# A four-layer modulated convolution folded into one kernel per sample: the order of the opening's loads and sums, low parts against GpSimd, one store behind copies, and the last sample in two banks

## Chip, core and metric

The kernel runs on one core of one Trainium2 chip. The metric is the device time of one execution in microseconds (us), the median of repeated runs. A profile of one execution is read with it; its time line starts at the first instruction.

## What is computed

The input is x, 128 samples of 64 channels by 1024 positions, and a style vector of 128 numbers per sample. Four convolution layers of 64 channels and three taps follow each other, each with weights that depend on the sample:

```python
s = style @ mw.T + mb                                   # per sample and input channel
weight = SCALE * w * s[:, None, :, None]
demod = lax.rsqrt(jnp.sum(weight * weight, axis=(2, 3)) + EPS)
weight = weight * demod[:, :, None, None]
# types: 'same', 'upsample' (transposed conv, stride 2, then blur),
#        'same', 'downsample' (blur, then stride 2); each adds its bias b
x = x + L0(x, cond_512, ...)
```

Everything is linear, so the four layers of a sample fold into one short filter, plus a constant and a correction at the ends of the sequence.

## The kernel before

**Filters.** For each group of four samples (g = 0 to 31) TensorE multiplies small matrices in seven units, `unit(g, u)`, u = 0 to 6: units 0 and 1 are the root products (Q3 by A2), 2 and 3 bring in B1, 4 to 6 bring in C. Their results are in PSUM banks `pg`. Between units VectorE scales a result with per-sample factors (`full`, L914, L916, L922, L931), ScalarE rounds it to the 32-bit format that TensorE takes at full rate (`high`, L624, L628) and VectorE forms the rest as a second such number (`low`, L939 to L949). Each product is thus three matmuls, high by high, high by low, low by high (`split_mm`, L182 to L184). The last units give the filter Wf with seven tap matrices (S0, W0, W1, S2, W2, W3, W4), whose high and low parts go into W (`w_high`/`w_low`, for group 0 and the first pair of it `pair_high`/`pair_low`, L643 and L1019). Nine SP transfers per group (`cross`, L231) copy parts of W to the other half of the partitions, each as soon as `s_wh` and `s_wl` say that the parts are ready.

**Samples.** For each sample b, `conv_shared(b)` makes a sum of three taps that both output halves share into `ps` (or a `pg` bank), 9 matmuls of 256 columns. ScalarE copies it twice into `py` (`shared_copy`, L592), `conv_rest(b)` adds five taps in 15 matmuls, and ScalarE writes the scaled result into T (`result`, L600). The input comes in pairs of samples n = b // 2: SP's `load(n)`, GpSimd's two differences (`columns(n)`, L846 and L847), ScalarE's high part (`x_high`, L586), and the low part (`x_low`) on GpSimd for the first three pairs (L851), on VectorE for the others (L906). T has two halves: `result` of pair n waits until `store(n - 2)` has landed. Samples 120 to 127 (from LAST) have no more units behind them; for the last group the copies are made in halves (`last_cross`).

**Order.** All queues are written out by hand, engine by engine; an engine runs its list in order and waits on semaphores. SP has one queue for loads, copies and stores. In the loop over groups (L287) it issues a load, a store, the nine copies of the next group, a load and a store. The opening works the same way: SP and ACT load constants; TensorE forms style products (`scale`, L477), energies (`energy`, L481) and the B1 sums (L499, in fp32, with the identity and three multiples of it that GpSimd makes at L813); ScalarE takes squares and roots (L659, L664), VectorE does three Newton steps on each root (`newton`, L1014 to L1017). `JUNK` matmuls (L529) fill the time before the first sample. VectorE's list ahead of the loop is L1059 to L1161.

## Time and profile before

| | us |
|---|---|
| median of 3 runs | 629.14 (628.71 to 630.32) |
| the profiled execution | 630.22 |
| its span | 628.4 |
| TensorE busy | 617.2 (98%) |
| VectorE busy | 527.8 (84%) |
| ScalarE busy | 437.2 (70%) |
| GpSimd busy | 243.4 (39%) |
| DMA queue of SP | 75.0% of 16 engines |

The span reaches from the first to the last instruction; the execution's own time has some 1.8 us more around it. A matmul's time in the profile contains its way through the pipeline, so rows of 0.28 us start every 0.12 us; whether TensorE loses time is seen from the starts. "Idle before" names what ended a wait, "issue" where no record of the profile does.

### The profile page before, as it was taken

Reading aid. Unit: us, or ns where it says so; the run is one execution under the profiler, and the core shown is the slowest. Engines: PE = TensorE matmul, PEld = TensorE weight load, DVE = VectorE, ACT = ScalarE, POOL = GpSimd, SP = SyncE. Lnnn points to the kernel's source line nnn. Section 1 sums busy time; section 2 is a strip of 40 time slices with the busy share of each in tenths; the row PEclk is TensorE's granted clock in tenths of the full one; section 3 lists DMA queues with packets and bytes.
Section 4 is the critical chain, followed back from the end, with each engine's and each line's share of the span. In section 5 each row is a group of like instructions: output and inputs, shape, how many; then the busy total and the mean of one; then the engine's idle time right before and its main releaser. Section 6 shows DMA issues by size and latency. Waiting matters only on the chain.

```text
span 628.4 us, 13021 instructions
## 1 busy us (share of the span) xinstructions
PE 617.2 (98%) x4849; PEld 603.8 (96%) x4849; DVE 527.8 (84%) x783; ACT 437.2 (70%) x730; POOL 243.4 (39%) x251
## 2 busy tenths in 40 slices
PE   8998999999999999999999999999999999999997
PEld 7888999999999999999999999999999999999997
DVE  5989878899988888888898887889788888888881
ACT  6658776767776776766776777676767677676673
POOL 5556434424424423433423433432442443343430
PEclk9999999999999999999999999999999999999999
DMA  6448977778968677887678787777897877798683
GB/s 195 133 105 207 251 190 205 214 196 217 243 173 235 203 223 199 228 220 188 209 210 230 205 227 206 204 220 200 206 252 166 237 204 220 197 239 219 188 234 136
DMA packets 154287, 129.38 MB, mean 206 GB/s; under 512 B 7025, under 2 KB 120625, under 8 KB 154225
## 3 DMA queue, kind: packets, MB, share of 16 engines
q1 hardware_dynamic: 153920, 128.29, 75.0%
q8 instruction: 39, 0.64, 0.4%
q10 hardware_dynamic: 304, 0.26, 0.2%
q14 instruction: 24, 0.19, 0.1%
HBM read 36.44 MB, written 33.75 MB: 112 GB/s over the span
## 4 chain that ended last, share of the span: by engine, by line
PE 94%; DVE 2%; ACT 1%; issue 1%; DMA 1%; POOL 0%; ACTq 0%; DVEq 0%
PE py L183 12%; PE py L184 12%; PE py L182 12%; PE pg L182 8%; PE pg L184 8%; PE pg L183 8%; PE ps L182 7%; PE ps L183 7%; PE ps L184 7%; PE pg L187 3%; PE pg L188 3%; PE pg L409 1%; PE pg L410 1%; PE pe L465 1%; DMA EYE<-in_eye 1%
## 5 line engine op out<-in xcount | busy, mean ns | idle before, releaser
L183 PE MATMUL py<-xl,W 128*128 128x256 f32 x640 | 181.7, 284 | 0.0
L184 PE MATMUL py<-xh,W 128*128 128x256 f32 x640 | 181.4, 283 | 0.0
L182 PE MATMUL py<-xh,W 128*128 128x256 f32 x640 | 181.1, 283 | 0.0
L846 POOL TENSOR_TENSOR X<-X 128x514 f32<-128x514 f32 x64 | 74.3, 1161 | 217.3 <-DMA X<-in_xin 199.2
L182 PEld LDWEIGHTS py<-xh,W 128*128 128x128 f32 x640 | 126.2, 197 | 0.2 <-issue 0.2
L184 PEld LDWEIGHTS py<-xh,W 128*128 128x128 f32 x640 | 126.1, 197 | 0.0
L183 PEld LDWEIGHTS py<-xl,W 128*128 128x128 f32 x640 | 125.6, 196 | 0.0
L592 ACT COPY py<-ps 128x512 f32<-128x512 f32 x123 | 70.5, 573 | 60.9 <-PE ps L184 60.5
L906 DVE TENSOR_TENSOR xl<-X,xh 128x1548 fp32r<-128x1548 f32 x61 | 108.2, 1773 | 1.1 <-ACT xh L586 1.0
L182 PE MATMUL ps<-xh,W 128*128 128x256 f32 x369 | 105.2, 285 | 1.8 <-issue 1.8
L183 PE MATMUL ps<-xl,W 128*128 128x256 f32 x369 | 104.8, 284 | 0.0
L184 PE MATMUL ps<-xh,W 128*128 128x256 f32 x369 | 104.6, 283 | 0.0
L600 ACT ACTIVATE T<-py,cv,DD 128x512 f32<-128x512 f32 x128 | 99.8, 779 | 6.3 <-PE py L184 6.3
L586 ACT CAST xh<-X 128x1548 fp32r<-128x1548 f32 x64 | 94.8, 1482 | 0.0
L847 POOL TENSOR_TENSOR X<-X 128x516 f32<-128x516 f32 x64 | 84.4, 1319 | 0.0
L830 POOL TENSOR_TENSOR Q3l<-Q3f,Q3h 128x256 fp32r<-128x256 f32 x31 | 24.4, 786 | 140.4 <-ACT Q3h L615 140.4
L182 PEld LDWEIGHTS ps<-xh,W 128*128 128x128 f32 x369 | 72.5, 196 | 2.4 <-issue 2.4
L635 ACT CAST W<-Wf 128x768 fp32r<-128x768 f32 x60 | 50.3, 839 | 33.8 <-PE py L184 24.4
L963 DVE TENSOR_TENSOR W<-Wf,W 128x768 fp32r<-128x768 f32 x60 | 67.4, 1149 | 7.1 <-ACT W L635 6.7
L183 PEld LDWEIGHTS ps<-xl,W 128*128 128x128 f32 x369 | 72.7, 197 | 0.0
L184 PEld LDWEIGHTS ps<-xh,W 128*128 128x128 f32 x369 | 72.6, 197 | 0.0
L628 ACT CAST Gh<-pg 128x512 fp32r<-128x512 f32 x64 | 37.8, 591 | 35.3 <-DVE pg L916 35.3
(194 smaller groups left out, 1416.3 us busy)
## 6 DMA issues: line engine op xcount, KB each, us to landing
X<-in_xin SPq DMA_DIRECT2D x64, 516.0 KB, 5.5
out<-T SPq DMA_DIRECT2D x63, 512.0 KB, 4.3
W<-W SPq DMA_DIRECT2D x60, 384.0 KB, 4.4
W<-W SPq DMA_DIRECT2D x93, 128.0 KB, 4.2
W<-M SPq DMA_DIRECT2D x90, 128.0 KB, 3.6
W<-W SPq DMA_DIRECT2D x30, 256.0 KB, 4.7
W<-W SPq DMA_DIRECT2D x7, 192.0 KB, 2.8
E<-in_ed SPq DMA_DIRECT2D x1, 768.0 KB, 7.7
```

Source lines behind the costliest of these rows:

```text
L182: eng.matmul(o, wh_, rh, start=first, stop=False, skip_group_check=onto)
L183: eng.matmul(o, wh_, rl, start=False, stop=False, skip_group_check=onto)
L184: return eng.matmul(o, wl_, rh, start=False, stop=last, skip_group_check=onto)
L586: act.copy(xh[:, n % XH], X[:, n % XR, :, 1:4]).then_inc(s_xh, 1)
L592: act.copy(py[b % YR][:, :].rearrange("p (e k) -> p e k", e=2), shared(b).unsqueeze(1).to_broadcast([128, 2, H])).then_inc(s_ae, 1)
L600: act.activation(T[:, n % TR, q].rearrange("p e k -> p (e k)"), py[b % YR][:, :], ACT.Identity, bias=cv[:, b:b + 1], scale=DD[:, L[3], b:b ...
L628: act.copy(Gh[:, :, 2 * u - 4:2 * u - 2], src).then_inc(s_gh, 1)
L635: act.copy(taps_of(g, 0, k), Wf[:, :, PARTS[k]]).then_inc(s_wh, 1)
L846: pool.tensor_tensor(x[:, :, 3, 0:XW - 1], x[:, :, 0, 1:XW], x[:, :, 1, 0:XW - 1], ALU.subtract)
L847: pool.tensor_tensor(x[:, :, 2], x[:, :, 0], x[:, :, 1], ALU.subtract).then_inc(s_s, 1)
L906: tt(xl[:, n % XH], X[:, n % XR, :, 1:4], r32(xh[:, n % XH]), ALU.subtract).then_inc(s_xl, 1)
L963: m = tt(taps_of(g, 1, k), Wf[:, :, PARTS[k]], r32(taps_of(g, 0, k)), ALU.subtract)
```

## The change

- **Loads of the opening.** b1 goes from fourth to second place on SP, eye from third to second on ACT.
- **Opening sums.** TensorE does the two scale products of layers 0 and 1 after the B1 sums, ScalarE the first root ahead of the second square, ScalarE and VectorE the B1 parts ahead of what needs those scale products; one Newton step moves ahead of the product of `full(0, 2)`.
- **First samples.** One of the two copies for the first tap goes out on ACT's queue; `first_shared` does the first tap of sample 0, then of sample 1, then the others. 10 filler matmuls, not 13.
- **Low parts.** The three `pair_low(1, k)` stand together, ahead of the wait for PP_K2; `w_low(1, 0)` stands behind `full(1, 6)`; `D10` stands later. GpSimd does `q3_low(2)` ahead of `x_low(1)` and then waits for `s_wl` to reach 4 before `columns(2)`. ScalarE does `q3_high(2)` and `q3_full(3)` earlier.
- **Near the end.** At g = 29 SP issues the nine copies and load(62) ahead of store(57).
- **Last sample.** Its shared sum is copied in two halves, into `py` and `ps`; results and stores of the halves are separate.

VectorE from the last low part of the root product of group 1 to the scaling of the filter. The names: Q2h high part and rest of the root product, W and M the low parts of the filter, kt and tmp the constant's, pg the products of unit 2 and 3, Wf the filter. Before:

```order
L191 TENSOR_TENSOR Q2h<-pg,Q2h 64x2x128
L1023 TENSOR_TENSOR W<-Wf,W 128x3x128
L1131 SCALAR_TENSOR_TENSOR kt<-pe,DD 64x128
L1132 SCALAR_TENSOR_TENSOR tmp<-kt,MS,S 64x128
L1023 TENSOR_TENSOR W<-Wf,W 128x3x128
L1025 TENSOR_TENSOR M<-Wf,M 128x128
L916 TENSOR_TENSOR pg<-pg,D10c 128x512 x2
```

and now:

```order
L191 TENSOR_TENSOR Q2h<-pg,Q2h 64x2x128
L1040 TENSOR_TENSOR W<-Wf,W 128x3x128 x2
L1042 TENSOR_TENSOR M<-Wf,M 128x128
L1149 SCALAR_TENSOR_TENSOR kt<-pe,DD 64x128
L1150 SCALAR_TENSOR_TENSOR tmp<-kt,MS,S 64x128
L933 TENSOR_TENSOR pg<-pg,D10c 128x512 x2
```

The second W part and the M part moved ahead of the two steps that wait for TensorE's constant.

SP in the turn of g = 29 and the start of g = 30, as the difference (X<-in_xin is a load, out<-T a store, the others copy W):

```order
 L228 DMA out<-T 128x2x512
 L223 DMA X<-in_xin 128x2x516
-L228 DMA out<-T 128x2x512
-L238 DMA W<-W 64x12x128
-L239 DMA W<-W 64x4x128
-L240 DMA W<-W 64x4x128
-L242 DMA W<-W 64x12x128
-L243 DMA W<-W 64x4x128
-L244 DMA W<-W 64x8x128
-L223 DMA X<-in_xin 128x2x516
-L246 DMA W<-M 64x4x128
```

```order
+L246 DMA W<-M 64x4x128
+L247 DMA W<-M 64x4x128
+L248 DMA W<-M 64x4x128
+L223 DMA X<-in_xin 128x2x516
+L228 DMA out<-T 128x2x512 x2
 L223 DMA X<-in_xin 128x2x516
```

The store that stood ahead of the copies now stands behind them and behind load(62), next to store(58).

```diff
@@ -27 +27 @@
 LAST = B - 2 * NG
-JUNK = 13
+JUNK = 10
 EPS = 1e-8 * (C * 9)
@@ -211 +211 @@
     for n, dst, src in (("m2", MS[:], m2),
+                        ("b1", b1w, b1.rearrange("p (s c) -> p s c", s=4)),
                         ("m301", M301, m301),
                         ("q3", q3s[:], q3.rearrange("p (k o) -> p k o", k=2)),
-                        ("b1", b1w, b1.rearrange("p (s c) -> p s c", s=4)),
                         ("a2", A2f, a2)):
@@ -282 +282 @@
     sp.dma_start(w[hi, S0:W1 + 1, :, 0, 1], w[lo, S0:W1 + 1, :, 0, 0]).then_inc(s_w0, 16)
-    sp.dma_start(w[lo, S0, :, 0, 1], w[hi, W0, :, 0, 0]).then_inc(s_w0, 16)
     sp.dma_start(w[lo, W1, :, 0, 1], w[hi, W0, :, 0, 0]).then_inc(s_w1, 16)
@@ -293 +292 @@
             last_cross(0)
-        if n:
+
+        late = g + 3 == NGR
+        if n and not late:
             store(n - 1)
@@ -298 +299 @@
         elif g + 1 < NGR:
-            cross(g + 1, 0)
-            cross(g + 1, 1)
-
-            if g == NGR - 3:
-                load(n + 1 + XR)
-            cross(g + 1, 2)
-        if n + 1 + XR < NQ and g != NGR - 3:
+            for k in range(3):
+                cross(g + 1, k)
+        if n + 1 + XR < NQ:
             load(n + 1 + XR)
+        if late:
+            store(n - 1)
         store(n)
@@ -311 +310 @@
     n = NQ - 1
-    for q in range(Q):
-        sp.wait_ge(s_y, Q * n + q + 1)
-        sp.dma_start(out[n * Q + q], T[:, n % TR, q]).then_inc(s_st[n % TR], 16)
+    for k, (q, e) in enumerate(((0, slice(0, 2)), (1, 1), (1, 0))):
+        sp.wait_ge(s_y, Q * n + k + 1)
+        sp.dma_start(out[n * Q + q][:, e], T[:, n % TR, q, e]).then_inc(s_st[n % TR], 16)
...
@@ -332 +331 @@
 -                if b == 0:
...
-            return
        if g == NGR - 1 and q == 0:
@@ -361 +344 @@
             pe.wait_ge(s_xl, n + 1)
-        if b > LAST or b == 2:
-            pe.wait_ge(s_ae, b - 1)
-        elif b == 1:
-            pe.wait_ge(s_ce, PLACE[0, 6] + 1)
-        elif b:
-            pe.wait_ge(s_ae, b)
+        pe.wait_ge(s_ae, b - 1 if b > LAST or b == 2 else b)
         taps(b, shared(b), XO, ((S0, True, False), (S2, False, False), (W4, False, True))).then_inc(s_a, 1)

+    def first_shared():
+
+        o = [shared(b) for b in range(Q)]
+        pe.wait_ge(s_h0, 1)
+        pe.wait_ge(s_l0, 1)
+        pe.wait_ge(s_w0, 16 * 2)
+        pe.wait_ge(s_xh, 1)
+        pe.wait_ge(s_xl, 1)
+        taps(0, o[0], XO, ((S0, True, False),))
+        pe.wait_ge(s_ce, PLACE[0, 6] + 1)
+        taps(1, o[1], XO, ((S0, True, False),))
+        pe.wait_ge(s_h0, 2)
+        pe.wait_ge(s_l0, 2)
+        pe.wait_ge(s_vh, 1)
+        pe.wait_ge(s_vl, 1)
+        taps(0, o[0], XO, ((S2, False, False),), k=1)
+        pe.wait_ge(s_vh, 2)
+        pe.wait_ge(s_vl, 2)
+        taps(0, o[0], XO, ((W4, False, True),), k=2).then_inc(s_a, 1)
+        taps(1, o[1], XO, ((S2, False, False), (W4, False, True)), k=1).then_inc(s_a, 1)
+
     def conv_rest(b):
@@ -374 +373 @@
             pe.wait_ge(s_vl, 3)
-        o = py[b % YR]
-        taps(b, o[:, H:2 * H], XO1, ((W1, False, False), (W3, False, True)), True)
-        taps(b, o[:, 0:H], XE0, ((W0, False, False), (W2, False, False), (W4, False, True)), True).then_inc(s_p, 1)
+        o = [py[b % YR][:, 0:H], py[b % YR][:, H:2 * H]]
+        if b == B - 1:
+            o[0] = ps[:, 0:H]
+        m = taps(b, o[1], XO1, ((W1, False, False), (W3, False, True)), True)
+        if b == B - 1:
+            m.then_inc(s_p, 1)
+            pe.wait_ge(s_ae, b + 2)
+        taps(b, o[0], XE0, ((W0, False, False), (W2, False, False), (W4, False, True)), True).then_inc(s_p, 1)

@@ -490 +494 @@
     scale(3, M301[:, 0:128]).then_inc(s_pp, 1)
-    scale(0, M301[:, 128:256])
-    scale(1, M301[:, 256:384]).then_inc(s_pp, 1)

@@ -500 +502 @@
     m.then_inc(s_pp, 1)
+    scale(0, M301[:, 128:256])
+    scale(1, M301[:, 256:384]).then_inc(s_pp, 1)
     for x in PROLOGUE[:2]:
@@ -529 +533 @@
         pe.matmul(py[i % YR][:, :], A2h[:, 0:128], A2h[:, :], start=True, stop=True)
-    conv_shared(0)
-    conv_shared(1)
+    first_shared()
     conv_rest(0)
@@ -577 +580 @@
     act.dma_start(WT[:, 0], wt2.rearrange("p (t m) -> p t m", t=3)).then_inc(s_in["wt2"], 16)
-    act.dma_start(WT[:, 1:4], wt.rearrange("p (l t m) -> p l t m", l=3, t=3)).then_inc(s_in["wt"], 16)
     act.dma_start(EYE[:], eye).then_inc(s_in["eye"], 16)
+    act.dma_start(WT[:, 1:4], wt.rearrange("p (l t m) -> p l t m", l=3, t=3)).then_inc(s_in["wt"], 16)

@@ -672 +675 @@
     act.activation(tmp[0:64, L[2]], scales[2][0:64], ACT.Square, bias=BB[0:64, 1, 2:3]).then_inc(s_ss, 1)
-    act.wait_ge(s_in["wt"], 16)
-    square(1, 4)
     act.wait_ge(s_pp, PP_E2)
     root(RR[:, L[2]], pe_[:, 0:128])
+    act.wait_ge(s_in["wt"], 16)
+    square(1, 4)
     act.wait_ge(s_in["a2"], 16)
@@ -683 +686 @@
     m.then_inc(s_q3h, 1)
-    act.wait_ge(s_pp, PP_S01)
-    for l in (2, 1):
-        act.activation(S[:, l], scales[l], ACT.Identity, bias=BB[:, 1, l:l + 1]).then_inc(s_sa, 1)
     act.wait_ge(s_pp, PP_B1)
@@ -690 +690 @@
              py[0][:, 0:5 * C].rearrange("p (m c) -> p m c", m=5).unsqueeze(2).to_broadcast([128, 5, 2, C])).then_inc(s_k0, 1)
+    act.wait_ge(s_pp, PP_S01)
+    for l in (2, 1):
+        act.activation(S[:, l], scales[l], ACT.Identity, bias=BB[:, 1, l:l + 1]).then_inc(s_sa, 1)
     for l in (0, 1):
@@ -713 +716 @@
     act.copy(W[lo, 0, W2, 0, 0, 1], Wf[hi, 0, W1])
+    act.wait_ge(s_h0, 1)
+    act.wait_ge(s_l0, 1)
+    act.dma_start(r32(W[lo, 0, S0, :, 0, 1]), r32(W[hi, 0, W0, :, 0, 0])).then_inc(s_w0, 16)
     pair_high(0, 1)
@@ -728 +734 @@
     x_high(1)
+    q3_high(2)
     high(1, 2)
     high(1, 3)
-    q3_high(2)
+    q3_full(3)
     act.wait_ge(s_sc, SC_CV)
@@ -744 +751 @@
     high(2, 1)
-    q3_full(3)
     q3_high(3)
@@ -795 +801 @@
         result(b - 2)
-        shared_copy(b)
+        if b < B - 1:
+            shared_copy(b)
+
+    b = B - 1
+    act.wait_ge(s_a, b + 1)
+    act.wait_ge(s_y, b - YR + 1)
+    act.copy(py[b % YR][:, H:2 * H], shared(b)).then_inc(s_ae, 1)
+    act.copy(ps[:, 0:H], shared(b)).then_inc(s_ae, 1)
     result(B - 2)
-    result(B - 1)
+    for k, (e, o) in enumerate(((1, py[b % YR][:, H:2 * H]), (0, ps[:, 0:H]))):
+        act.wait_ge(s_p, b + 1 + k)
+        act.activation(T[:, b // Q % TR, b % Q, e], o, ACT.Identity, bias=cv[:, b:b + 1],
+                       scale=DD[:, L[3], b:b + 1]).then_inc(s_y, 1)

@@ -868 +884 @@
     identity(1)
-    x_low(1)
     q3_low(2)
+    x_low(1)
+    pool.wait_ge(s_wl, 4)
     for b in range(B):
@@ -1052 +1069 @@
         full(g, 5)
-        w_low(g, 0)
         dve.wait_ge(s_id, g + 1)
@@ -1057 +1073 @@
         full(g, 6)
+        w_low(g, 0)

@@ -1081 +1098 @@
     lone_low(dve, Q3h[hi, :, 1], Q3f[hi, :, 1]).then_inc(s_q3l, 1)
-    dve.wait_ge(s_sa, 2)
-    reached(tt(D21[:], S[:, 1], S[:, 2], ALU.mult))
     dve.wait_ge(s_k0, K_B1)
@@ -1088 +1103 @@
        r32(B1hw[:, C:11 * C]).rearrange("p (m h c) -> p m h c", m=5, h=2), ALU.subtract).then_inc(s_b1, 1)
+    dve.wait_ge(s_sa, 2)
+    reached(tt(D21[:], S[:, 1], S[:, 2], ALU.mult))
     dve.wait_ge(s_sc, SC_D21)
@@ -1100 +1117 @@
     link(newton(0, 2, py[0][:, 0:128], ps[:, 256:384]))
+    link(newton(1, 2, None, ps[:, 256:384]))
     dve.wait_ge(s_k, 1)
     full(0, 2)
-    link(newton(1, 2, None, ps[:, 256:384]))
     link(newton(2, 2, None, ps[:, 256:384]))
@@ -1128 +1145 @@
     low(1, 1)
-    pair_low(1, 0)
+    for k in range(3):
+        pair_low(1, k)
     dve.wait_ge(s_pp, PP_K2)
@@ -1132 +1150 @@
     reached(stt(out=tmp[lo, 2], in0=kt[lo], scalar=BB[lo, 0, 2:3], in1=S[lo, 3, :], op0=ALU.add, op1=ALU.mult))
-    pair_low(1, 1)
-    pair_low(1, 2)
     full(1, 2)
@@ -1147 +1163 @@
     w_low(1, 2)
-    tt(D10[:], DD[:, L[0]], DD[:, L[1]], ALU.mult)
     dve.wait_ge(s_k0, K_B0)
@@ -1160 +1175 @@
     low(3, 1)
+    tt(D10[:], DD[:, L[0]], DD[:, L[1]], ALU.mult)
     dve.wait_ge(s_xl, 3)
```

## Rows read from the trace of the kernel before

**Rows 1.** The page, part 1: busy time, share of the span, instructions of each engine.

```profile
PE 617.2 (98%) x4849; PEld 603.8 (96%) x4849; DVE 527.8 (84%) x783; ACT 437.2 (70%) x730; POOL 243.4 (39%) x251
```

**Rows 2.** Timeline of the opening: start, us, engine, line, operation [idle before, releaser].

```profile
7.03 1.06 PE L477 MATMUL ps<-MS,Wf 128*128 128x128 f32 x4
8.40 0.77 PE L499 MATMUL py<-b1s,EYE 128*128 128x128 f32 x2 [0.32 <-POOL Wf L813]
11.38 0.56 PE L182 MATMUL pg<-Q3h,A2h 128*128 128x256 f32 x1
...
6.54 1.71 POOL L813 TENSOR_SCALAR Wf<-EYE 128x128 f32<-128x128 f32 x3 [4.40 <-DMA EYE<-in_eye]
```

**Rows 3.** DMA issues by line: engine, operation, number, size, median us to landing.

```profile
W<-W SPq DMA_DIRECT2D x7, 192.0 KB, 2.8
W<-W SPq DMA_DIRECT2D x11, 64.0 KB, 2.5
...
out<-T SPq DMA_DIRECT2D x2, 256.0 KB, 2.0
...
EYE<-in_eye ACTq DMA_DIRECT2D x1, 64.0 KB, 4.5
```

**Rows 4.** Timeline before the first tap sum, TensorE and SP.

```profile
24.46 3.13 PE L529 MATMUL py<-A2h 128*128 128x512 f32 x13
28.00 0.37 PE L182 MATMUL ps<-xh,W 128*128 128x256 f32 x1 [0.41 <-issue]
...
25.29 0.63 SPq L283 DMA_DIRECT2D W<-W  x1
```

**Rows 5.** Timeline from 33 to 50 us, TensorE, VectorE and GpSimd.

```profile
39.60 0.47 PE L182 MATMUL pg<-Gh,Ch 128*128 128x512 f32 x1 [0.61 <-DVE Gl L945]
...
49.22 0.36 PE L182 MATMUL pg<-Q2h,B1h 128*128 128x256 f32 x1 [1.65 <-DVE Q2h L191]
...
34.22 3.29 DVE L1025 TENSOR_TENSOR M<-Wf,M 128x128 fp32r<-128x128 f32 x1
...
43.06 1.86 DVE L963 TENSOR_TENSOR W<-Wf,W 128x768 fp32r<-128x768 f32 x1
...
33.63 3.73 POOL L851 TENSOR_TENSOR xl<-X,xh 128x1548 fp32r<-128x1548 f32 x1 [0.57 <-ACT xh L586]
...
43.00 1.10 POOL L847 TENSOR_TENSOR X<-X 128x516 f32<-128x516 f32 x1
```

**Rows 6.** Timeline from 584 to 603 us, TensorE, VectorE, ScalarE and SP.

```profile
601.07 0.37 PE L182 MATMUL ps<-xh,W 128*128 128x256 f32 x1 [1.39 <-issue]
...
584.38 1.81 DVE L963 TENSOR_TENSOR W<-Wf,W 128x768 fp32r<-128x768 f32 x2
...
595.83 0.79 ACT L600 ACTIVATE T<-py,cv,DD 128x512 f32<-128x512 f32 x1
596.50 1.48 ACT L586 CAST xh<-X 128x1548 fp32r<-128x1548 f32 x1
599.78 0.92 ACT L656 CAST W<-Wf 128x384 fp32r<-128x384 f32 x2 [1.79 <-DVE Wf L958]
...
602.45 0.57 ACT L592 COPY py<-ps 128x512 f32<-128x512 f32 x1 [1.07 <-PE ps L184]
...
586.63 0.60 SPq L238 DMA_DIRECT2D W<-W  x1
...
596.38 0.60 SPq L228 DMA_DIRECT2D out<-T  x1
```

**Rows 7.** Timeline of SP, the first copy of the group before, at g = 28.

```profile
567.11 0.60 SPq L238 DMA_DIRECT2D W<-W  x1
```

**Rows 8.** The store behind those copies and a load, issued at 576.6: landing.

```profile
DMA to landing us min/median/max: 5.5/5.5/5.5
```

**Rows 9.** All 56 stores issued from 60 to 580 us: landing.

```profile
DMA to landing us min/median/max: 2.9/4.7/6.5
```

**Rows 10.** Timeline of ScalarE, the last result.

```profile
625.16 0.78 ACT L600 ACTIVATE T<-py,cv,DD 128x512 f32<-128x512 f32 x1 [1.03 <-PE py L184]
```

More of the change, by code:

```diff
@@ L163, in build @@
             sem(n) for n in ("pp", "ch", "eps", "ms", "sq", "ss", "rr", "sc", "k0", "b1", "j", "ey", "vh", "vl", "k"))
-        PP_S2, PP_E2, PP_S3, PP_S01, PP_B1, PP_E01, PP_E3, PP_K1, PP_K2, PP_K3 = range(1, 11)
+        PP_S2, PP_E2, PP_S3, PP_B1, PP_S01, PP_E01, PP_E3, PP_K1, PP_K2, PP_K3 = range(1, 11)
         SC_S3, SC_D32, SC_D21, SC_D, SC_K2, SC_K3, SC_CV = range(1, 8)
@@ L311, in _ @@
             n = NQ - 1
-            for q in range(Q):
-                sp.wait_ge(s_y, Q * n + q + 1)
-                sp.dma_start(out[n * Q + q], T[:, n % TR, q]).then_inc(s_st[n % TR], 16)
+            for k, (q, e) in enumerate(((0, slice(0, 2)), (1, 1), (1, 0))):
+                sp.wait_ge(s_y, Q * n + k + 1)
+                sp.dma_start(out[n * Q + q][:, e], T[:, n % TR, q, e]).then_inc(s_st[n % TR], 16)
             for i in range(TR):
-                sp.wait_ge(s_st[i], 16 * (len(range(i, NQ, TR)) + (Q - 1 if i == n % TR else 0)))
+                sp.wait_ge(s_st[i], 16 * (len(range(i, NQ, TR)) + (2 if i == n % TR else 0)))
             sp.wait_ge(s_eo, 16)
@@ L332, in conv_shared @@
                 n, q = divmod(b, Q)
-                if b == 0:
-                    pe.wait_ge(s_h0, 1)
-                    pe.wait_ge(s_l0, 1)
-                    pe.wait_ge(s_w0, 16 * 2)
-                    pe.wait_ge(s_xh, 1)
-                    pe.wait_ge(s_xl, 1)
-                    taps(b, shared(b), XO, ((S0, True, False),))
-                    pe.wait_ge(s_h0, 2)
-                    pe.wait_ge(s_l0, 2)
-                    pe.wait_ge(s_vh, 1)
-                    pe.wait_ge(s_vl, 1)
-                    taps(b, shared(b), XO, ((S2, False, False),), k=1)
-                    pe.wait_ge(s_vh, 2)
-                    pe.wait_ge(s_vl, 2)
-                    taps(b, shared(b), XO, ((W4, False, True),), k=2).then_inc(s_a, 1)
-                    return
                 if g == NGR - 1 and q == 0:
@@ L577, in _ @@
             act.dma_start(WT[:, 0], wt2.rearrange("p (t m) -> p t m", t=3)).then_inc(s_in["wt2"], 16)
+            act.dma_start(EYE[:], eye).then_inc(s_in["eye"], 16)
             act.dma_start(WT[:, 1:4], wt.rearrange("p (l t m) -> p l t m", l=3, t=3)).then_inc(s_in["wt"], 16)
-            act.dma_start(EYE[:], eye).then_inc(s_in["eye"], 16)
             def x_high(n):
@@ L672, in _ @@
             act.activation(tmp[0:64, L[2]], scales[2][0:64], ACT.Square, bias=BB[0:64, 1, 2:3]).then_inc(s_ss, 1)
+            act.wait_ge(s_pp, PP_E2)
+            root(RR[:, L[2]], pe_[:, 0:128])
             act.wait_ge(s_in["wt"], 16)
             square(1, 4)
-            act.wait_ge(s_pp, PP_E2)
-            root(RR[:, L[2]], pe_[:, 0:128])
             act.wait_ge(s_in["a2"], 16)
@@ L868, in _ @@
             identity(1)
+            q3_low(2)
             x_low(1)
-            q3_low(2)
+            pool.wait_ge(s_wl, 4)
             for b in range(B):
```

## The prediction

> **What bounds the kernel now.** I read the page first. TensorE's matmul row is busy for 98% of the span [rows 1], and its granted clock is in the top tenth in all 40 slices of the page (the 2.4 GHz level), so time can only go where TensorE's issue is interrupted, before its stream starts, or after its last matmul. The waits view shows only a handful of entries for it, so I went through the TensorE timeline and looked for matmuls that start more than 0.12 us after the one before (0.12 us is the regular step of the 256-column ones). After the opening there are four interruptions: first tap sum at 28.00, first matmul of sample 1's product at 39.60 (0.61 idle), root product at 49.22 (1.65 idle, 1.80 against the regular step) and first shared sum of sample 120 at 601.07 (1.39 idle, 1.54 against the step) [rows 4 to 6]. Between 49.22 and 599.5 there is none. A gain before 49.22 therefore shifts everything behind it, if what the other engines and the DMAs deliver moves with it.
>
> **Term A: the opening, 0.35 us.** The B1 sums (L499) start at 8.40 [rows 2], released by GpSimd's three scaled identities, which waited for EYE. EYE was issued as ACT's third transfer and took 4.5 us; a 64 KB transfer elsewhere takes 2.5 [rows 3]. It is now second, one issue of some 0.6 us earlier, at 1.3, so it should land at 3.8 to 5.8, and GpSimd's 1.71 us follow. Then B1 can start where the two scale products of layers 0 and 1 started, at 7.03, and these (1.06 us) follow it. The step from 8.40 to the first root product at 11.38 is 2.98 us; 7.03 + 2.98 + 0.96 (1.06 less the overlap of two neighbours) = 10.97, 0.4 earlier. A little of that may be lost where more of the root product runs before the clock is up: its matmuls there step by 0.2 us, later ones by 0.12. VectorE's B1 low part and products follow TensorE there; one Newton step now fills VectorE's wait before the next product. Ends: 0 (m301, now behind b1, or wt, now behind EYE, lands late and holds the scale product or a square) and 1.0 (all of 8.40 minus 7.03, less what B1's own chain needs). I take 0.35, near the sum.
>
> **Term B: first tap sum, 0.42 us.** Two copies gate it, issued by SP one after the other; the second goes out at 25.29 and takes 2.5 us, 27.8, and TensorE starts at 28.00 [rows 3, 4]. Now ACT issues that copy at 24.6, beside SP's first; the first (192 KB, 2.8 us) is then last, at 27.4. The gain is 0.4. ACT's issue costs its queue 0.6 us before pair_high(0,1), which itself waits for VectorE there until 25.76: hidden. The ends are 0.1 and 0.45. The Trainium skill, "DMA: Bandwidth & Descriptors", section "Issuing engines are not separate DMA queues", speaks against more: transfers issued from several engines run on the same 16 DMA engines and interleave, so only issue time is saved. By that page the second copy's 64 KB would push out the first's landing, and B would be nearer 0.1. Three filler matmuls fewer (0.24 each) cost nothing while TensorE waits for this copy: fillers end at 24.46 - 0.35 + 2.5 = 26.6, the data is there at 27.2. Sample 1's first taps ahead of sample 0's second fill the time until the low parts are ready, worth no more than 0.1, and are counted at nothing.
>
> **Term C: 0.77 us, the wait at 39.60.** VectorE's M<-Wf,M at L1025 took 3.29 us for 128 columns; it starts at 34.22 and ends with GpSimd's xl at 33.63 + 3.73 [rows 5]. The products at L916 queue behind it, then ScalarE's high parts and the low ones, and TensorE waits 0.61. The change puts all three pair_low(1,k) before the wait on PP_K2, so they run near 31.4 to 33.0, ahead of that xl, which also moves behind q3_low(2). Then L916 waits for its own product only and is done by 36.0; TensorE arrives at 37.9 with everything there. I book 0.61 idle plus the restart, 0.77, whole.
>
> **Term D: 1.0 us of the 1.80 at 49.22.** Here the chain is VectorE's: from the product at 39.60, through L922, L963, L957, L931, L914 to the low part that releases TensorE. In it L963 starts at 43.06 and takes 1.86; GpSimd's columns end at 43.00 + 1.10 = 44.10, 1.04 later [rows 5]. The new wait on s_wl holds these columns until VectorE has done its low part, now after full(1,6). The chain loses 1.0 and keeps the rest: TensorE, which was there at 49.22 - 1.80 = 47.42, now is at 47.42 - 0.35 - 0.42 - 0.77 = 45.88, and is released at 49.22 - 1.54 - 1.0 = 46.68. So 0.8 of the wait stays. Queued behind GpSimd's new wait are columns(2), q3_low(3) and x_low(2); sample 4 needs the last at about 56.4, and columns end near 46.6 and x_low(2) near 50: covered by 6 us. Ends: 0.5 and 1.3.
>
> **Term E: the copies ahead of a store, a loss of 0.5 us.** The wait at 601.07 is for the last of nine W copies of group 30. At g = 29 SP now leaves store(57) and load(62) until these are issued: the first goes when its low part is ready, halfway through the L963 pair of 584.38 and so near 585.35, instead of at 586.63 [rows 6], and two transfers of half a megabyte are out of its way. I expect the last to land near 598, a little before TensorE wants it at 599.5, and the 1.54 us to go. But store(57) frees the half of T that result(118) writes. That result started at 595.83 [rows 6]. In group 28 the step from the first copy's issue at 567.11 to the landing of the store behind copies and load is 576.6 + 5.5 - 567.11 = 15.0 us [rows 7, 8]; with one store less ahead I allow 13.5 to 15. So store(57) lands at 598.9 to 600.4, and result(118) waits 3 to 4.5 us. Behind it on ScalarE are x_high(61), two last_high (0.92), result(119) and shared_copy(120), and TensorE's rest of sample 120 waits for that copy: 0.67 + 1.38 + 0.83 + 0.70 + 0.57 + 0.15 for the signal = 4.3 us from result(118)'s start (each row's time less the tenth by which the next overlaps it), so 603.2 to 604.7. Before, that rest started at 601.07 + 2.26 (18 matmuls and a restart) = 603.33. The edit is worth between +0.1 and -1.4; with the landing at 599.5 it costs 0.5. What is late next is the rest of sample 120, for a store's landing and no longer for copies. Ends: a gain of 1.54, a loss of 1.4.
>
> **Term F: the tail, 0.3 us.** The last result (0.78 us [rows 10]) is halved, its first half runs beside the last nine matmuls, in its own bank. At most 0.39 is saved, less the fixed part; the last store is half as large, but its 2.0 us [rows 3] is already short of what the 64 KB copies take. I take 0.3, ends 0.1 and 0.6. The copy of shared(127) in two is ready before it is wanted.
>
> **Sum.** 0.35 + 0.42 + 0.77 + 1.0 - 0.5 + 0.3 = 2.34 us. The profiled execution took 630.22 us (span 628.4, 1.8 around it), so a profile of the change should show a span near 626.1. That execution is 1.1 above the median of the runs, 629.14; from the median I get **626.8 us**. About 0.3%, 1.9 us, is what a measurement of this kernel can tell from no change: 627.25 is the border.
>
> **Rivals.**
> *The store lands in time* (chance 0.12). If store(57) lands by 597.4, result(118) costs TensorE nothing and E is +1.54 instead of -0.5: 629.14 - 4.4 = 624.8. For it: 56 stores took 2.9 us at the least [rows 9], and issued at 594.5 that would do. Against: this one is behind nine copies and a load, and their median is 4.7.
> *The lock moves instead of going* (0.13). VectorE's w_low(1,1), w_low(1,2) and edge_in near 46.6 to 49 now meet GpSimd's q3_low(3) and x_low(2). If edge_in falls behind x_low(2), over 3 us long as the xl row in [rows 5], full(2,2) comes near 52, and TensorE waits about 1.7 us at the product of group 2: 628.5. The M row above is just such a case. The Trainium skill, "SBUF — State Buffer", section "Who interferes with whom", says that a VectorE instruction with two SBUF inputs and a GpSimd one that reads SBUF block each other for a whole instruction, whoever is first; edge_in and w_low have two such inputs. By that page it hangs on tenths of a microsecond who wins; the row of M agrees with it.
> *The opening gives nothing* (0.18). m301 or wt lands late, A and half of B fall away: 629.14 - 1.8 = 627.3.
> *Slower than before* (0.07): the stall of term E is larger. It decides from the point where store(57) lands after 601.8, since each microsecond beyond 599.0 goes straight to TensorE, and the other terms give 2.84. Issued at 596.38, where SP now has the store after those copies [rows 6], and landing in 6.5 us, the longest of the stores [rows 9], it would be 602.9, E -3.9: 629.14 - 2.84 + 3.9 = 630.2. Against it: with a store and a load fewer ahead SP should be there about two issues sooner.
> The forecast's own case has 0.50; its range alone is 625.8 to 627.8.
>
> **How the numbers follow.** Faster by more than the border: most of the forecast's case (0.40), all of the first rival, half of the third's 0.18 and a little of the lock's: 0.64. Within it: 0.31. Slower: the far part of the last rival and what I overlook, 0.05. The range 624.7 to 628.6 takes in the early store and the lock, and leaves out the slower case and the ends where several terms fail together.
>
> **What would show it.** A: B1 sums start near 7.1. B: first tap sum near 27.2. C: no VectorE row of 128 columns above 1 us before 40, and no idle before sample 1's products. D: L963's successor takes under 1 us, idle before the root product falls from 1.65 to about 0.7 and sits near 46.7. E: no "issue" wait before sample 120's shared sum, but a gap of 1 to 3 us before its rest, and ScalarE idle before result(118), released by the store. F: last activation 0.5 us. The forecast is wrong if the stream between these points is no longer gapless, if the clock rises later than before, or if the root product comes later than 47.5.

## Result and profile after

The changed kernel takes 632.77 us (median of 22 runs, 628.33 to 634.32), the kernel before 629.18 (22 runs, 628.21 to 630.32): ratio 1.0049, 95% interval 1.0035 to 1.0063. It is 3.6 us slower where 2.3 us less were forecast, and it lies above the range (624.7 to 628.6). The profiled execution took 632.22 us, span 630.3.

The page, part 1, of the changed kernel [rows 1 before]:

```profile
PE 616.7 (98%) x4846; PEld 602.6 (96%) x4846; DVE 530.7 (84%) x783; ACT 437.2 (69%) x732; POOL 242.5 (38%) x251
```

TensorE is as busy as before; the two microseconds are waits again. The waits view of the changed kernel, TensorE alone (what waited, for what: us in total, times, longest):

```profile
PE py L182 <- ACT py L595: 2.8, 1, 2.8
PE pg L182 <- DVE Gl L962: 1.7, 2, 0.9
...
PE ps L182 <- issue: 1.4, 2, 1.2
PE pe L462 <- DVE b1s L987: 1.2, 1, 1.2
PE pg L182 <- DVE Q2h L191: 1.0, 2, 0.6
```

Of the lines shown, two have no counterpart before: the first, and L462's for b1s. The timeline of TensorE at the points of the terms (a line of the kernel before is up to 17 higher here):

```profile
7.17 0.77 PE L501 MATMUL py<-b1s,EYE 128*128 128x128 f32 x2
10.72 0.36 PE L182 MATMUL pg<-Q3h,A2h 128*128 128x256 f32 x1
27.08 0.36 PE L182 MATMUL ps<-xh,W 128*128 128x256 f32 x1 [1.17 <-issue]
46.53 0.36 PE L182 MATMUL pg<-Q2h,B1h 128*128 128x256 f32 x1 [0.63 <-DVE Q2h L191]
52.05 1.24 PE L462 MATMUL pe<-b1s,E 128*128 128x192 f32 x6 [1.21 <-DVE b1s L987]
54.21 0.47 PE L182 MATMUL pg<-Gh,Ch 128*128 128x512 f32 x1 [0.92 <-DVE Gl L962]
56.99 0.38 PE L413 MATMUL pg<-Gh,Ch 128*128 128x256 f32 x1 [0.21 <-DVE Q2l L956]
605.63 0.39 PE L182 MATMUL py<-xh,W 128*128 128x256 f32 x1 [2.83 <-ACT py L595]
```

Up to 50 us it goes as forecast and better. The root product of group 2 comes at 46.53, 2.69 us before its time in [rows 5] (forecast: 46.68), the wait before sample 1's product is gone, and the one before the root product fell from 1.65 to 0.63. Then TensorE waits three times for VectorE, and the lead of 2.69 becomes a lag of 0.38. The cause is a pair on VectorE and GpSimd:

```profile
47.68 0.96 DVE L982 TENSOR_TENSOR M<-Wf,M 128x256 fp32r<-128x256 f32 x1
48.57 3.43 DVE L987 TENSOR_TENSOR b1s<-XE,S 128x256 f32<-128x256 f32 x1
52.02 1.30 DVE L933 TENSOR_TENSOR pg<-pg,D10c 128x512 f32<-128x512 f32 x2
...
48.44 3.27 POOL L867 TENSOR_TENSOR xl<-X,xh 128x1548 fp32r<-128x1548 f32 x1
```

edge_in (L987) starts 0.13 us after GpSimd's x_low(2) and ends 0.29 us after that ends. In the kernel before it came first and was short (VectorE, then GpSimd):

```profile
51.07 0.41 DVE L970 TENSOR_TENSOR b1s<-XE,S 128x256 f32<-128x256 f32 x1
...
52.16 3.21 POOL L851 TENSOR_TENSOR xl<-X,xh 128x1548 fp32r<-128x1548 f32 x1
```

It is the sight of M in [rows 5], on another instruction. Behind it the product L933, the low parts of G and with them TensorE are late.

From 60 to 585 us the lag stays at 0.38; at 590 it becomes 0.94 in this trace, at a first tap sum of group 29, for which the profile names no cause ("issue", 0.27 us); no term has this loss of 0.56 us, and two other traces of the changed kernel's order at group 29 have one of 0.2 and 0.5 there. The last part, ScalarE and SP (last result and store against [rows 6]):

```profile
601.45 0.78 ACT L603 ACTIVATE T<-py,cv,DD 128x512 f32<-128x512 f32 x1 [4.59 <-DMA out<-T]
602.12 1.47 ACT L589 CAST xh<-X 128x1548 fp32r<-128x1548 f32 x1
603.49 0.92 ACT L659 CAST W<-Wf 128x384 fp32r<-128x384 f32 x2
604.32 0.78 ACT L603 ACTIVATE T<-py,cv,DD 128x512 f32<-128x512 f32 x1
604.99 0.59 ACT L595 COPY py<-ps 128x512 f32<-128x512 f32 x1
...
586.46 0.60 SPq L238 DMA_DIRECT2D W<-W  x1
...
595.82 1.01 SPq L228 DMA_DIRECT2D out<-T  x2
```

The wait of [rows 6] for the last copy is gone. But store 57 goes out at 595.8 and lands 5.5 us later, result(118) waits 4.59 us for it, and the chain of term E follows: TensorE stands 2.83 us at the rest of sample 120. The lag ends at 2.42. After the start of the last matmul 3.04 us are left, before 3.56. So the two profiled executions differ by 2.69 - 3.07 - 0.56 - 1.48 + 0.52 = -1.9 us, which is the whole difference of their spans.

### The profile page after: what moved, and what is told of

It is laid out like the page before. It is cut to its first block, busy times and chain, and to the rows that moved or that the text cites. A ratio compares the mean times of both kernels' runs of the same rounds, so it can differ in the third digit from the quotient of the medians.

```text
span 630.3 us, 13020 instructions
## 1 busy us (share of the span) xinstructions
PE 616.7 (98%) x4846; PEld 602.6 (96%) x4846; DVE 530.7 (84%) x783; ACT 437.2 (69%) x732; POOL 242.5 (38%) x251
## 4 chain that ended last, share of the span: by engine, by line
PE 89%; DVE 5%; ACT 2%; SPq 1%; issue 1%; DMA 1%; ACTq 0%; DVEq 0%
PE py L182 11%; PE py L183 11%; PE py L184 11%; PE pg L182 8%; PE pg L184 8%; PE pg L183 8%; PE ps L182 7%; PE ps L183 7%; PE ps L184 7%; PE pg L187 3%; PE pg L188 3%; PE pg L413 1%; PE pg L414 1%; DMA out<-T 1%; PE pe L469 1%
## 5 line engine op out<-in xcount | busy, mean ns | idle before, releaser
L862 POOL TENSOR_TENSOR X<-X 128x514 f32<-128x514 f32 x64 | 72.7, 1135 | 222.9 <-DMA X<-in_xin 201.8
L846 POOL TENSOR_TENSOR Q3l<-Q3f,Q3h 128x256 fp32r<-128x256 f32 x31 | 25.7, 827 | 134.9 <-ACT Q3h L618 134.9
```

The costliest lines, as they stand in the source:

```text
L862: pool.tensor_tensor(x[:, :, 3, 0:XW - 1], x[:, :, 0, 1:XW], x[:, :, 1, 0:XW - 1], ALU.subtract)
```

## Experiments

Medians of one group of runs stand beside 22 to 27 runs of the kernel before on the same chip (629.25 to 629.48). "Lead" is how much earlier than in the first trace of the kernel before a matmul starts.

### The two stalls, apart and together

The changed kernel once more without an edit (first), with SP's order of group 29 as before (second), with one wait on GpSimd (third), with both (fourth). The wait holds x_low(2) until edge_in is done:

```
                if b == Q:
+                    pool.wait_ge(s_ed, 1)
                    x_low(2)
```

> The changed kernel once more, beside the experiments. Its trace shows two stalls that the kernel before has not: TensorE stands 2.83 us at the rest of sample 120 (released by a store's landing through ScalarE), and from 52 to 57 us it loses 3.07 us because VectorE's scaling of the edge columns takes 3.43 us. Theory S (two additive stalls): runs spread with the landing of that one store, so from about 628 (it lands in 3 us) to 634, mean clock unimportant. Rival K: the stall at the end of the kernel also lets TensorE's granted clock fall for some us; then a run with a mean clock of 1.000 is near 628.5 to 632 and one with 0.997 some 1.5 to 2 us above it, and a trace with 0.997 shows the clock fall next to 603 us. Expected median 632.5.

Measured: 634.14 us (630.49 to 635.08), ratio 1.006 [1.0042, 1.0079]. That is 4.7 us above the kernel before on this chip, where the first comparison had 3.6.

> The changed kernel with the order of SP's transfers at group 29 as before (store 57 ahead of the copies, load before the last copy); all else kept. Theory S: the 2.83 us stall goes and the old wait of 1.39 us at the first tap sum of sample 120 comes back; the trace lost 1.48 us there, so 632.22 - 1.5 = 630.7 for a profile like the last, median about 631.2. Rival K (stall plus clock): 629.2 to 629.7, all runs at a mean clock of 1.000, and a much narrower spread of runs, like the kernel before's. A third view, that the loss from 52 to 57 us is a chance of one execution: below 627.5.

Measured: 630.15 us (627.92 to 631.21), ratio 1.0005 [0.9992, 1.0019]. The wait for the last copy is back (1.05 us); the three waits at 52 to 58 us are there as before, a loss of 3.1.

> The changed kernel plus one wait on GpSimd: its low part of the third pair of samples (3.3 us) starts only after VectorE's first scaling of the edge columns. Theory: the two lock each other; with the wait VectorE's instruction falls to about 0.6 us, the stalls of 1.21, 0.92 and 0.21 us from 52 to 57 us go, TensorE gains 2.5 to 3.1 us: median 629.5 to 630.2. The late stall at the rest of sample 120 stays (2.8 us in a trace). Rival: VectorE's instruction is slow in itself or TensorE waits for the next thing (the low part of sample 4, held longer now): gain under 1 us, median 631.8 or more.

Measured: 630.79 us (628.09 to 631.72), ratio 1.0011 [0.9998, 1.0024]. The three waits are gone from its trace; the late one is there (2.76 us).

> Both edits: SP's order of group 29 as before, and GpSimd's low part behind the edge scaling. If the two stalls are all that went wrong, the sum of my terms without term E and with a gain of 2.5 to 3 us in the opening is left: TensorE 2.7 us ahead at 49 us, old wait at 601, tail 0.5 shorter: 629.2 - 2.7 - 0.5 = 626.0, range 625.5 to 626.7, narrow spread, clock 1.000. If more is lost elsewhere (a clock that falls in the opening because fewer filler matmuls run): 627.5 or more with a mean clock below 1.000.

Measured: 627.82 us (627.07 to 628.79), ratio 0.9967 [0.9955, 0.9979].

Undoing the store's order is worth 4.0 us alone and 3.0 us beside the other edit, the wait on GpSimd 3.4 and 2.3, the two together 6.3, so each is worth 1.0 less once the other is there. Both stalls are real, and without them the change is 1.7 us faster than the kernel before by the medians. The timeline of the kernel with both edits, VectorE and GpSimd:

```profile
49.50 0.41 DVE L988 TENSOR_TENSOR b1s<-XE,S 128x256 f32<-128x256 f32 x1
...
50.05 3.22 POOL L867 TENSOR_TENSOR xl<-X,xh 128x1548 fp32r<-128x1548 f32 x1 [0.75 <-DVE b1s L988]
```

The same instruction takes 0.41 us where it took 3.43, as soon as x_low(2) isn't under way. The timeline marks no wait of TensorE between 48 and 598 us there.

The wait does not remove every lock. In the trace with the wait alone (third run) the pair W<-Wf,W now meets GpSimd's column differences and takes 3.11 us, where the trace with both edits has 1.81; ScalarE and TensorE follow, and TensorE's lead falls from 2.39 to 1.71:

```profile
59.03 3.11 DVE L981 TENSOR_TENSOR W<-Wf,W 128x768 fp32r<-128x768 f32 x2
...
59.52 1.81 POOL L863 TENSOR_TENSOR X<-X 128x516 f32<-128x516 f32 x1
...
63.92 0.40 PE L182 MATMUL py<-xh,W 128*128 128x256 f32 x1 [0.41 <-ACT py L595]
```

Of the six traces with this wait two have that loss, 0.7 and 0.6 us (this one and the first with a third T buffer, below), and four have none: in the trace with both edits it is GpSimd's instruction that is long (2.48 us from 59.95 on).

Part of the loss is TensorE's clock. In the trace of the repeated change (634.18 us) the windows view, TensorE and its granted clock (the column after POOL), reads:

```profile
48.00:52.00 4.00, 2.96 (x25) 2.76 (x24) 4.00 (x2) 0.04 (x1) 3.92 (x3) 1.00 0.74 177
...
54.00:56.00 2.00, 1.66 (x5) 1.41 (x6) 1.94 (x5) 0.32 (x2) 0.70 (x2) 0.60 1.03 133
56.00:58.00 2.00, 2.00 (x9) 1.71 (x9) 1.61 (x5) 2.00 (x7) 0.00 (x0) 0.54 0.98 346
58.00:60.00 2.00, 2.00 (x19) 2.00 (x19) 1.97 (x3) 1.81 (x2) 1.48 (x2) 1.00 0.95 364
...
604.00:606.00 2.00, 0.00 (x0) 0.00 (x0) 1.46 (x3) 2.00 (x5) 0.00 (x0) 1.00 0.00 0
606.00:608.00 2.00, 1.86 (x13) 1.86 (x14) 1.99 (x3) 1.75 (x5) 0.00 (x0) 0.84 0.64 147
608.00:610.00 2.00, 2.00 (x11) 2.00 (x11) 1.46 (x4) 1.18 (x2) 0.42 (x1) 0.50 0.66 149
610.00:612.00 2.00, 2.00 (x16) 2.00 (x15) 0.99 (x1) 1.99 (x4) 1.74 (x2) 0.80 0.61 177
```

After each stall the granted clock goes from 2.4 to 1.2 GHz (1.00 to 0.5) for some 3 us, with 9 and 11 matmuls in 2 us instead of 19. This trace loses 4.0 us from 50 to 60 instead of 3.07, and 2.8 instead of 1.48 at the end. Of the changed kernel's own 22 runs only three have a mean clock of 1.000, the profiled one (632.22 us) among them; the others have 0.997 or 0.994. So the trace that was read first lacks a part of the loss that most runs have. Against rival K of the first expectation, the clock doesn't sort the runs by itself: those at 0.997 took 630.1 to 634.3 us. The two others at 1.000 took 628.33 and 628.51, inside the forecast's range; no trace shows which stalls they were spared.

### Each order edit by itself

The change of group 29 alone, on the kernel before:

```
-                if n:
+
+                late = g + 3 == NGR
+                if n and not late:
                     store(n - 1)
...
-                    cross(g + 1, 0)
-                    cross(g + 1, 1)
-
-                    if g == NGR - 3:
-                        load(n + 1 + XR)
-                    cross(g + 1, 2)
-                if n + 1 + XR < NQ and g != NGR - 3:
+                    for k in range(3):
+                        cross(g + 1, k)
+                if n + 1 + XR < NQ:
                     load(n + 1 + XR)
+                if late:
+                    store(n - 1)
                 store(n)
```

> The kernel before with one edit alone: at group 29 SP issues the three copies and the load ahead of store 57. So far the edit cost 4.0 us in the medians, about 1.5 us in a trace whose clock stayed up and 2.8 in two whose clock fell after the stall. Here TensorE comes 2.5 us later to the place than in the changed kernel with the edge wait, and store 57 hangs on SP's queue, whose times hang on TensorE too, so the stall should be the same: theory (stall of 2.8 us for the 1.39 us one, and the clock falling in most runs): +2 to +3.5 us on the kernel before, 631.5 to 633, mean clock 0.997 in most runs. Rival (the cost comes from an interplay with the other edits): within 0.7 us of the kernel before.

Measured: 631.98 us (630.92 to 632.42), ratio 1.0038 [1.0025, 1.0051]; mean clock of its trace 0.997. The edit alone costs 2.6 us by the medians; the lead in its trace goes from +1.14 before the stall to -0.17 behind it and, with the clock at half (0.50 from 604 to 606 us), to -1.76 at the end. ScalarE and TensorE there:

```profile
599.31 0.78 ACT L600 ACTIVATE T<-py,cv,DD 128x512 f32<-128x512 f32 x1 [4.54 <-DMA out<-T]
...
603.50 0.52 PE L182 MATMUL py<-xh,W 128*128 128x256 f32 x1 [2.79 <-ACT py L592]
```

The next has the store first, all copies, then the load. It is the changed kernel with the wait on GpSimd; against its order of group 29 as before, the edit is:

```
-                    if g == NGR - 3:
-                        load(n + 1 + XR)
                     cross(g + 1, 2)
-                if n + 1 + XR < NQ and g != NGR - 3:
+                if n + 1 + XR < NQ:
                     load(n + 1 + XR)
```

> As the kernel with both edits (627.82), but at group 29 SP issues store 57, then all three copies, then the load; before, the load went out ahead of the last copy. Theory (the wait at the first tap sum of sample 120 is the last copy behind half a megabyte of load): that wait falls from 0.65 to 1.4 us to under 0.3, result(118) does not wait for store 57, gain 0.5 to 1.0: median 626.9 to 627.3. Rival (it waits for the copy because SP comes late to it, held by the store's own wait): no gain, 627.8, the wait stays at 0.65 or more.

Measured: 627.92 us (626.13 to 628.74), ratio 0.9972 [0.9963, 0.9982], no gain over the kernel with both edits (0.9967). Half right: the wait at sample 120 went, and one of 1.0 us came at sample 122. GpSimd and VectorE there:

```profile
598.55 1.37 POOL L858 TENSOR_TENSOR X<-X 128x514 f32<-128x514 f32 x1 [9.65 <-DMA X<-in_xin]
599.89 1.42 POOL L859 TENSOR_TENSOR X<-X 128x516 f32<-128x516 f32 x1
...
600.26 2.67 DVE L920 TENSOR_TENSOR xl<-X,xh 128x1548 fp32r<-128x1548 f32 x1
```

The later load makes GpSimd's column differences late, and they now overlap VectorE's low part (2.67 us; 1.76 in the trace with both edits). That this is what the wait at sample 122 comes from is likely; the profile gives it as "issue".

The new wait on the low parts of group 1, taken out (group 29 as before, no wait for edge_in):

```
-            pool.wait_ge(s_wl, 4)
```

> As the kernel with group 29's order undone (630.15), but without the new wait of GpSimd on the low parts of group 1. Theory (that wait is what pushed GpSimd's third low part onto VectorE's edge scaling): GpSimd runs earlier, VectorE's edge scaling takes about 0.4 us instead of 3.43 and the 3 us of stalls from 51 to 58 us go; in return term D is lost, the root product of group 2 waits about 1 us more: shift of TensorE against the kernel before -0.7 to -1 at 60 us, median 628.2 to 629. Rival (the lock falls on another VectorE instruction in any case, as before at 43 us): 629.5 or more.

Measured: 629.32 us (627.02 to 631.05), ratio 0.9997 [0.9983, 1.001]. Not as either said. In its trace edge_in takes 0.41, x_low(2) waits for ScalarE's x_high(2) and starts at 50.04, and the root product has no wait; instead TensorE waits 1.04 for ScalarE's W parts at 42.5, and from 28 to 50 us it gains 1.3 us (1.8 with the wait and edge_in first). Runs from 627 to 631 in one kernel show that the order isn't fixed here; the trace is one of the good ones. That the bad ones have the lock is likely and not shown. In this trace GpSimd was free for x_low(2) at 49.17, ahead of edge_in at 49.37. It started behind edge_in because x_high(2) came at 48.41, not at 47.28 as in the second run, behind a copy that waited 1.0 us for TensorE. So the new wait isn't what brings x_low(2) forward. The rows say what does: ScalarE's Q3h of group 3 was at 49.38 before and is at 45.37 now, x_high(2) at 50.42 and now 46.42, since q3_full(3) went earlier on ScalarE and TensorE itself was 2.7 us ahead. So x_low(2) went from 52.16 to 48.44, 3.7 us, but VectorE's edge_in, in the middle of its chain, from 51.07 to 48.57, only 2.5: the two met.

SP issues the second copy of group 0 again (term B undone; both stalls undone):

```
+            sp.dma_start(w[lo, S0, :, 0, 1], w[hi, W0, :, 0, 0]).then_inc(s_w0, 16)
...
-            act.dma_start(r32(W[lo, 0, S0, :, 0, 1]), r32(W[hi, 0, W0, :, 0, 0])).then_inc(s_w0, 16)
```

> As the kernel with both edits (627.82), but the second copy of group 0's first tap sum is issued by SP behind its first, as in the kernel before, and not by ScalarE. In four traces of the changed issue the step from the end of the fillers to the first tap sum was 0.1 to 0.2 us longer than before, so the two transfers only share the 16 DMA engines: gain of 0 to 0.3 us in the trace, no difference in the medians (627.5 to 628.1). Rival (my term B): 0.4 us slower at the first tap sum, against the first root product.

Measured: 627.19 us (626.81 to 628.08), ratio 0.9965 [0.9952, 0.9978]. From the first filler to the first tap sum it is 3.57 us here, 3.43 to 3.62 in all seven traces in which SP issues both (mean 3.56), and 3.62 to 3.84 in the seven with ScalarE's issue (mean 3.69). Term B is a loss of 0.1 in the traces; the medians show no difference (ratio 0.9965 here, 0.9967 with ScalarE's issue).

### The opening

> The kernel before, unchanged, for a second trace of its opening. In the trace of before the first root product starts at 11.38 us and TensorE's granted clock comes up at about 12.6; in one other kernel with the same opening the product started at 10.76. Theory (the clock comes up at a time that varies from execution to execution, and the 0.9 us by which the changed kernel led in its trace was mostly that): first root product between 10.7 and 11.4, and TensorE at 28 us up to 1.2 us earlier than in the first trace. Rival (11.38 is the rule): 11.3 to 11.5 again.

Measured: 629.09 us (628.65 to 630.37), ratio 1.0002 [0.9992, 1.0012]; but its opening is 1.1 us earlier than in the first trace. TensorE in the first trace of the kernel before, and then in this one:

```profile
12.17 0.41 PE L182 MATMUL pg<-Q3h,A2h 128*128 128x256 f32 x1
12.38 0.37 PE L183 MATMUL pg<-Q3l,A2h 128*128 128x256 f32 x1
```

```profile
10.76 0.36 PE L182 MATMUL pg<-Q3h,A2h 128*128 128x256 f32 x1 [0.15 <-DVE Q3l L1080]
10.96 0.28 PE L183 MATMUL pg<-Q3l,A2h 128*128 128x256 f32 x1
11.07 0.29 PE L184 MATMUL pg<-Q3h,A2l 128*128 128x256 f32 x1
```

Steps of 0.21 us at 12 us in the one, of 0.12 at 11 us in the other. The windows view gives a granted clock of 1.00 for both openings and so doesn't show this; but where it gives 0.50, at 608 to 610 us in the trace of the repeated change, the same matmuls step by 0.21 too. Read so, the clock comes up at 12.6 us in the one execution and by 11.0 in the other. The Trainium skill says that the moment of the rise varies from run to run of one kernel ("TensorE: Matmul & The Clock Gate", "Part 1: The HAM clock gate"); these traces agree that it varies, but by 1.6 us at least, where the page gives half a microsecond either way; here the measurement decides.

The clock isn't all of the 1.1 us. EYE lands 0.55 us earlier in the second trace (GpSimd's identities start at 5.99, not 6.54), and VectorE's low part of Q3, which the first root product waits for, starts 0.56 us earlier; first trace, then second:

```profile
10.75 0.43 DVE L1080 TENSOR_TENSOR Q3l<-Q3f,Q3h 128x256 fp32r<-128x256 f32 x1
```

```profile
10.19 0.42 DVE L1080 TENSOR_TENSOR Q3l<-Q3f,Q3h 128x256 fp32r<-128x256 f32 x1
```

> The kernel before with the edits of the opening alone (term A): EYE second on ScalarE's queue, b1 second on SP's, B1 sums ahead of the scale products, one Newton step earlier; second copy, fillers and all the rest as before. My term A said 0.35 us; eight traces of the changed opening have the first root product at 10.72 to 11.29, two of the old one at 11.38 and 10.76. Theory (nothing but the variation of clock and first landings): ratio 1.000, within 0.1%. Rival (a real gain of 0.35 to 0.9): ratio 0.9986 to 0.9994, which the trace would show as a first root product at 10.7 or below.

The edit, on the kernel before:

```
             for n, dst, src in (("m2", MS[:], m2),
+                                ("b1", b1w, b1.rearrange("p (s c) -> p s c", s=4)),
...
             act.dma_start(WT[:, 0], wt2.rearrange("p (t m) -> p t m", t=3)).then_inc(s_in["wt2"], 16)
+            act.dma_start(EYE[:], eye).then_inc(s_in["eye"], 16)
...
             m.then_inc(s_pp, 1)
+            scale(0, M301[:, 128:256])
+            scale(1, M301[:, 256:384]).then_inc(s_pp, 1)
```

with the old places of these lines removed, and the order on ScalarE and VectorE that goes with it. Measured: 629.25 us, ratio 1.0004 [0.9992, 1.0016]. First root product in three traces of the old opening: 11.38, 10.76, 10.76; in eleven of the new: 10.63 to 11.29, and both means are 10.97. Term A is nothing that can be seen. The first link of it came: the B1 sums start at 7.13 to 7.58 in the eleven, at 7.89, 7.89 and 8.40 in the three. But Q3's low part starts at 10.06 to 10.19 in all of the fourteen but the first trace, under either order, and ends 0.42 later, so the root product has nothing to gain below 10.5.

### What the store waits for: a third T buffer

Both kernels of this part have the changed order of group 29, the wait on GpSimd and SP's second copy; the first differs from the changed kernel by these two and by:

```
-TR = 2
+TR = 3
```

> The best kernel so far (both edits, copy by SP: 627.19) with the changed order of group 29 (copies, load, then store 57) and with a third T buffer, so that result(118) does not need store 57. Theory (the whole loss of term E is the wait for T): the stall of 2.8 us at the rest of sample 120 and the clock's fall go; but the load behind the copies comes late for GpSimd's column differences and VectorE's low part of sample 122, as in the kernel with the load last, where TensorE waited 0.96 us: 626.8 to 627.6. Rival (the stores and copies are late in themselves): a stall over 1.5 us at 120 stays, 629 or more.

Measured: 627.29 us (626.88 to 628.69), ratio 0.9973 [0.9961, 0.9985], clock 1.000. result(118) starts at once. A wait of 1.29 us is left at the rest of sample 120, which has another cause: two sums of VectorE that take 0.42 each in most places are long beside GpSimd's late column differences, and ScalarE waits 1.12 us for the second:

```profile
597.71 1.29 POOL L861 TENSOR_TENSOR X<-X 128x516 f32<-128x516 f32 x1
...
596.75 1.28 DVE L973 TENSOR_TENSOR Wf<-Wf 128x256 f32<-128x256 f32 x1
598.04 1.23 DVE L974 TENSOR_TENSOR Wf<-Wf 64x256 f32<-64x256 f32 x1
```

And the second, with the load back ahead of the last copy:

```
                     cross(g + 1, 0)
                     cross(g + 1, 1)
+                    if late:
+                        load(n + 1 + XR)
                     cross(g + 1, 2)
```

> As the last one (third T buffer), but the load stays ahead of the last copy as in the kernel before, and only store 57 goes behind the copies. Theory: the copies go out when their low parts are ready, 0.6 to 1.1 us sooner, the wait of 0.65 us before the first tap sum of sample 120 goes and none comes at sample 122: 0.7 us better than 627.19, so 626.4 to 626.8 and a span of 624.3 to 624.8. Rival (the load ahead of the last copy alone makes that wait): the wait of 0.6 us stays, 627.2.

Measured: 626.87 us (626.11 to 627.47), ratio 0.996 [0.9948, 0.9973], span 624.3: the lowest median of all, 2.4 us below the kernel before. Its interval overlaps that of the kernel with two T buffers, SP's old order and SP's copy (0.9965), so that the third buffer is worth more than the old order isn't shown. No wait at the tap sums of sample 120 or 122; the one at the rest of 120 is 0.42:

```profile
599.64 0.39 PE L182 MATMUL py<-xh,W 128*128 128x256 f32 x1 [0.42 <-ACT py L600]
```

## Why the prediction was wrong

- **The step that failed first:** the sum took terms C and D as a lead that TensorE keeps, with VectorE and GpSimd clear of each other behind 49 us, and left the rival "the lock moves instead of going" out of it. I gave that rival 0.13 and 1.7 us; it came in all three traces with the change's order there, at the place and time named (the product behind edge_in starts at 52.02, forecast "near 52"), and cost 3.1 us, 4.0 when the clock fell. I priced the first wait only: behind it the G low parts and the Q2 low part made TensorE wait twice more. And I left its chance to chance, though rows could say more: with ScalarE's Q3h and x_high(2) followed to their new times, x_low(2) moves further forward than edge_in. The Trainium skill's rule ("SBUF — State Buffer", "Who interferes with whom") that whoever is first holds the other for the whole instruction agrees with this pair: 3.43 beside 3.27 us, and 0.41 without.
- **Term E** (forecast -0.5, end -1.4) was -1.5. The kernel with E alone gives it in the time of the kernel before: first copy at 584.35 + 1.15 = 585.5 (forecast 585.35), result(118) started, as store 57 had landed, at 599.31 + 1.15 = 600.5, so 15.0 us, the full step of group 28; I had allowed 13.5 to 15 for a store fewer ahead. Of the 15.0 us SP's issues take 9.4 (586.46 to 595.82 in the first trace of the change), the landing the rest. Mechanism, place and chain were right; the stall lay at the far end of the working's own bounds or 0.1 us beyond, and the middle was the wrong choice.
- **What no term had**: the granted clock fell behind the late stall in three of its four traces. It costs some 1.3 us more at the end (2.8 to 2.9 in the three against 1.48), and 1 us more after the lock in one of the three traces with the lock. With 1.29 us of stall (the third T buffer) it stays at 1.00. "Slower than before" had the right sign and place with 0.07, but by a landing after 601.8; it landed by 600.5, and the loss needed the clock and the lock beside it.
- **Term A** 0.35: nothing (rival "the opening gives nothing", 0.18). The first trace of the change seemed to show 0.9 at the first tap sum; two more traces of the old opening say that this was the variation of the clock's rise and of EYE's landing. The number in [rows 2] was the late case. The step that failed is the 2.98 us from the B1 sums to the root product, carried over as one piece: its end hangs on VectorE's low part of Q3, which didn't move.
- **Term B** 0.42: -0.1. The Trainium skill's rule ("DMA: Bandwidth & Descriptors", "Issuing engines are not separate DMA queues"), by which the term would be near 0.1, was nearer than my sum. The fillers were no matter: TensorE stood idle 1.17 us at that point. The new order of the first taps, counted at nothing, costs 0.1 to 0.2: from the first tap sum to the first product with B1 behind it are 5.15 to 5.17 us in the ten traces that have it, 4.96 to 5.05 in the four others.
- **Term C** 0.77: 0.84 to 0.86 in every trace with it. **Term D** 1.0: 1.03. **Term F** 0.3: 0.5; 0.2 of it is the shorter last result (0.56 us, before 0.78), 0.3 is what follows it, where the last store is half as large.

Together: 0.84 + 1.03 + 0.5 - 0.1 - 3.1 - 1.5 - 1.3 = -3.6 us; measured -3.6. That these agree so well is partly luck: the parts come from single traces, the sum leaves out the first taps, the loss at 590 us and the fall after the lock, and by the same parts the kernel with both edits should gain 2.3 us where its median gains 1.7.

Open: what decides whether the clock falls after the waits at 52 to 57 us (it did in one of the three traces that have them) and after the late stall (three of four), and what the changed kernel's fastest runs were spared. No run settles these.

## What to carry to other kernels

When edits move one engine earlier, follow the other engine of a locking pair to its new time too, and pin their order with a wait where they come close; a wait of one line turned 3.4 us into 0.4. Then look for the next pair: here it cost 0.7 us some ten microseconds later in one trace. A store that frees a buffer is on the path of whoever writes that buffer next: before it is put behind other issues, count the issuing engine's time per transfer (0.6 to 1.5 us each here), or give it a buffer more. And one trace is one opening: two traces of the same kernel were 1.1 us apart at 28 us, so a difference of that size needs several.

## What the runs showed of the hardware

- A TensorE stall of 2.6 to 2.8 us in a kernel that is otherwise 98% busy was followed by a stretch at half clock (granted 0.50 to 0.58 over 2 us) in three of four traces, the waits of 1.2 and 0.9 us close together in one of three (0.54), and single waits of 1.0 to 1.9 us after the opening in none.
- Two kinds of VectorE instructions with both operands in SBUF (b1s<-XE,S and the sums of Wf) took 3.43 us instead of 0.41, and 1.28 and 1.23 instead of 0.42, beside GpSimd. A pair of W<-Wf,W took 3.11 us instead of 1.81.
- When two engines issued two copies at the same time, the matmul that needs both started 3.69 us after the first filler in the mean of seven traces; when one engine issued them 0.7 us apart, 3.56 us.
